# Moving the capacity mask of a routed MLP three tiles later, and laying its one-hots out with the token column innermost

## The reference, cut to what matters

```python
xn  = layernorm(x)                                   # x: 16 x 512 x 256
h   = scan(lam, xn @ B_w.T)                          # state space layer, 64 states
aff = xn @ waff.T / (|xn| * |waff|)                  # 8 experts
cap = clip(floor(S * sigmoid(mean(aff) - threshold)), 4, S)
top = one_hot(argmax(aff))                           # each token has one expert ...
kept = rank of the token in its expert's row < cap   # ... which keeps only its best cap tokens of a batch row
for each expert e:  out += gelu((xn * mask_e) @ W1[e] + b1[e]) @ W2[e] + b2[e]   # for ALL tokens
y = x + (h @ C_w.T + D * xn) + out
```

## Time and profile before

| what | value |
|---|---|
| time, median of 3 runs | 661.86 us (659.16 to 662.46) |
| the profiled execution | 663.84 us, its span 662.1 us |
| PE busy | 589.7 us (89%) |
| DVE busy | 512.2 us (77%) |
| POOL busy | 462.6 us (70%) |
| ACT busy | 337.3 us (51%) |

### The profile page before, as it was taken

One profiled execution on the slowest core, in us unless ns is written; L12 is line 12 of the kernel. 1 busy time (PEld: TensorE's weight loads), 2 busy tenths in 40 slices (PEclk: granted clock), 3 DMA queues, 4 the chain that ended last, 5 costly groups with the idle time before them and its releaser, 6 DMA issues.

```text
span 662.1 us, 16027 instructions
## 1 busy us (share of the span) xinstructions
PE 589.7 (89%) x4597; PEld 497.0 (75%) x4598; DVE 512.2 (77%) x974; ACT 337.3 (51%) x635; POOL 462.6 (70%) x625
## 2 busy tenths in 40 slices
PE   2988888858945599999999999999999999999994
PEld 1655555546834499898988888989898989898983
DVE  5789989799998979987667768676767676767672
ACT  5776868825799235644433435353535353535340
POOL 1999997920038838888776768787777787788453
PEclk9988868776997799999999999999999999999998
DMA  8985757611801134512212112212112212210100
GB/s 308 413 346 173 253 208 266 230 75 43 274 18 33 40 97 153 169 57 74 72 57 70 54 53 66 75 50 79 49 44 71 67 48 67 63 60 24 51 29 2
DMA packets 33584, 72.58 MB, mean 110 GB/s; under 512 B 6519, under 2 KB 19088, under 8 KB 33552
## 3 DMA queue, kind: packets, MB, share of 16 engines
q1 hardware_dynamic: 21488, 46.67, 19.7%
q0 software_dynamic: 11232, 25.20, 12.4%
q10 hardware_dynamic: 832, 0.31, 0.2%
HBM read 50.64 MB, written 27.00 MB: 117 GB/s over the span
## 4 chain that ended last, share of the span: by engine, by line
PE 69%; DVE 16%; ACT 7%; issue 6%; DMA 1%; POOL 1%; DVEq 0%; SPq 0%; ACTq 0%; POOLq 0%
PE ps_bu L820 10%; PE ps_bu L818 10%; PE ps_bu L819 10%; PE ps_t L793 5%; PE ps_y L795 5%; PE ps_t L794 5%; PE ps_y L794 5%; PE ps_t L795 5%; PE ps_y L793 5%; ACT area L494 2%; PE ps_y L662 2%; PE ps_bu L648 2%; PE ps_t L630 2%; ACT work L565 1%; PE ps_g L777 1%
## 5 line engine op out<-in xcount | busy, mean ns | idle before, releaser
L820 PE MATMUL ps_bu<-area,ring 128*128 x624 | 170.1, 273 | 1.5 <-issue 1.4
L818 PE MATMUL ps_bu<-area,ring 128*128 x624 | 170.1, 273 | 0.3
L819 PE MATMUL ps_bu<-area,ring 128*128 x624 | 170.1, 273 | 0.0
L1247 DVE SCALAR_TENSOR_TENSOR ring<-ring,h_scale 128x512 f16<-128x512 f32 x156 | 117.2, 751 | 5.6
L434 POOL DMA_INDIRECT out<-ring,idx_b x78 | 96.9, 1243 | 19.1 <-issue 14.7
L372 POOL TENSOR_TENSOR small<-ones 128x1 f32<-128x1 f32 x156 | 48.1, 308 | 86.8 <-DVE work L1161 33.4
L420 POOL DMA_INDIRECT work<-xn_rows,idx_x x78 | 87.1, 1117 | 27.1 <-issue 23.9
L444 POOL DMA_INDIRECT work<-base_rows,idx_b x78 | 92.3, 1183 | 18.0 <-issue 15.8
L596 ACT ACTIVATE ring<-ps_t,b1t,inv_in 128x256 f32<-128x256 f32 x156 | 79.2, 560 | 44.7 <-PE ps_t L795 42.4
L596 ACT ACTIVATE ring<-ps_y,b1t,inv_in 128x256 f32<-128x256 f32 x156 | 77.8, 562 | 45.9 <-PE ps_y L795 22.8
L1244 DVE TENSOR_SCALAR ring<-ring,h_scale 128x512 f16<-128x512 f32 x156 | 77.9, 499 | 23.4 <-issue 13.2
(11 more groups left out here) (267 smaller groups left out, 1085.0 us busy)
## 6 DMA issues: line engine op xcount, KB each, us to landing
ring<-L_ffn_W SPq DMA_DIRECT2D x14, 1024.0 KB, 6.4
xn_rows<-area SPq DMA_DIRECT2D x8, 1024.0 KB, 9.4
base_rows<-area SPq DMA_DIRECT2D x8, 1024.0 KB, 7.3
area<-L_attn_u SPq DMA_DIRECT2D x7, 1024.0 KB, 18.2
work<-L_ffn_W SPq DMA_DIRECT2D x5, 1024.0 KB, 9.0
work<-xn_rows,idx_x POOLq DMA_INDIRECT x78
work<-base_rows,idx_b POOLq DMA_INDIRECT x78
out<-ring,idx_b POOLq DMA_INDIRECT x78
```

The lines of the kernel that those rows point to most:

```text
L818: t.matmul(dst, hh, wh, start=(c == 0), stop=False)
L819: t.matmul(dst, hh, wl, start=False, stop=False)
L820: last = t.matmul(dst, hl, wh, start=False, stop=(c == C - 1))
L1247: v.scalar_tensor_tensor(out=hlo[p][:, cs], in0=h32[:, cs], scalar=h_scale[:, bass.ds(e, 1)], in1=hhi[p][:, cs], op0=ALU.mult, op1=ALU.sub ...
```

## The change

1. One-hots are stored with the token column innermost (128 x l x 16 in place of 128 x 16 x l), compared against a replicated counter `irep` that POOL writes once, and all operands are 16-bit. PE reads them with a stride of 16 elements (32 bytes).
2. The first affinity work is in another order: PE turns the affinity rows first, DVE makes the search key ahead of the one-hot of the expert, and PE computes zero rows 0 and 1 ahead of the count products.
3. The second key of the search is made by POOL. Tables of ACT are asked for ahead by two 128x1 ACTIVATEs.
4. ACT's second search is interleaved: after turn 4 three `zero_rows` copies, after turn 5 `split_x` of tile 0 and the last copy, after turn 7 all of step 0, after turn 9 all of step 1.
5. `result` is cut in two: `drained` (L1255) and the rest. Tiles 0 to 2 are drained unmasked; `kept_rows` stands in step 3 and `kept_slots` at its end, the mask is there in step 4. The late W2 units are split in steps 4 to 7 and not 2 to 5.
6. Their DMAs wait for `slots_ok` and not for `mask_ok`. `PEEL` is 10. Two low parts (units 10 and 11) come after the largest values of units 12 to 15.

```diff
-        lo16 = part(area, (UNITS - 4) * UW, T * P // 2).bitcast(F16).rearrange("p (t l) -> p t l", l=P)
+        lo16 = [part(area, (UNITS - 4) * UW + n * TG * P // 2, TG * P // 2).bitcast(F16).rearrange("p (l t) -> p l t", t=TG)
+                for n in range(4)]
...
-                    last = t.matmul(ps_num[:, g * NS:(g + 1) * NS], lo16[:, g * TG + i, :], planes[g][:, i, :],
+                    last = t.matmul(ps_num[:, g * NS:(g + 1) * NS], lo16[g][:, :, i], planes[g][:, :, i],
...
-                link(v.tensor_tensor(planes[g], same(NS), of(hi16, NS), ALU.is_equal))
+                link(v.tensor_tensor(planes[g], irep[:, 0:NS, :], of(hi16[:, cols], NS), ALU.is_equal))
...
+            pool.wait_ge(s["low_ok"], 1)
+            pool.wait_ge(s["hi_found"], 1)
+            g.tensor_scalar(search[:, 4:5], search[:, 0:1], -1.0, None, ALU.mult)
+            link(g.tensor_scalar(key_hi, key_hi, search[:, 0:1], 2.0 ** 17, ALU.add, ALU.mult))
+            g.memset(search[:, 0:1], -(2.0 ** 15 - 0.5))
+            g.tensor_tensor(key_hi, key_hi, low_half, ALU.add).then_inc(s["key_lo_ok"], 1)
...
+            for m in range(5, 8):
+                gates = rows_in(m, m % 4, gates)
+            for m in range(5, 8):
+                gates = out_and_base(m - 5, m - 3, (m + 3) % 4, (m + 1) % 4, gates)
...
             def second_half(n):
-                if n == 8:
-                    for i in range(E // 2):
+                if n == 4:
+                    for i in range(3):
                         zero_rows(i)
-                if n == 10:
+                if n == 5:
                     split_x(0, 0)
+                    zero_rows(3)
+                if n == 7:
+                    act.wait_ge(s["wsum_ok"], UNITS)
+                    act.wait_ge(s["scales_ok"], 1)
+                    step(0, 0)
+                if n == 9:
+                    step(1, 1)
...
             zero_row(0)
             zero_row(1)
             pe.wait_ge(s["oh_ok"], 1)
...
                 up(j, p)
-                if isinstance(j, int) and j == 0:
+                if first == 0:
                     late_bounds()
+                if first == 3:
                     kept_rows()
-                if isinstance(j, int) and j == 1:
+                if first == 4:
+                    pe.wait_ge(s["mask_ok"], 1)
+                    rows_t(5, 1, 2)
+                if first > 0:
+                    down(j - 1, 1 - p)
+                if first == 3:
+                    pe.wait_ge(s["kept_read"], 1)
+                    rows_t(4, 0, 2)
                     kept_slots()
-                if not (isinstance(j, int) and j == 0):
-                    down(j - 1, 1 - p)
...
+            x_low(1, 1)
+            h_parts(0, 0)
+            late_scales()
+            x_low(2, 0)
+            h_parts(1, 1)
+            out_scales()
+            drained(0, 0)
+            x_low(3, 1)
+            kept()
+            h_parts(2, 0)
+            drained(1, 1)
+            kept_places()
+            x_low(4, 0)
+            h_parts(3, 1)
+            kept_mask()
+            dve.wait_ge(s["mask_ok"], 1)
+            dve.wait_ge(s["c_ok"], E)
+            result(0, 0, 0)
+            result(1, 1, 0)
+            drained(2, 0)
```

More of the change, by code:

```diff
@@ L407, in is_tile, with rows_in, out_and_base @@
                 return not isinstance(j, int) or 0 <= j < NT
[L409 to L424, removed]
+            def rows_in(m, r, gate_no):
+                wait(pool, s["f_xt"], m - 1)
+                gate(gate_no)
+                g.tensor_copy(idx_x[:, 2 * r:2 * r + 2], idx_all[:, bass.ds(m * 2, 2)]).then_inc(s["ix"], 1)
+                pool.wait_ge(s["ix"], m + 1)
+                gate(gate_no + 1)
+                for h in range(2):
+                    g.indirect_dma_start(out=xg[r % 2][:, h * D:(h + 1) * D], out_offset=None, in_=xn_dram,
+                                         in_offset=bass.IndirectOffsetOnAxis(
+                                             ap=idx_x[:, 2 * r + h:2 * r + h + 1], axis=0),
+                                         bounds_check=bound, oob_is_err=False).then_inc(gx[r % 2], 16)
+                return gate_no + 2
+            def out_and_base(t_out, t_base, ro, rb, gate_no):
                 if is_tile(t_out):
@@ L599, in step @@
             def step(j, p):
[L600 to L604, removed]
+                if isinstance(j, int) and j in (3, 4):
+                    hidden(j)
+                    split_x(j + 1, 1 - p)
+                else:
+                    split_x(j + 1, 1 - p)
+                    hidden(j)
+                if isinstance(j, int) and 4 <= j < 4 + LATE:
+                    act.wait_ge(s["w_late"], 16 * (j - 3))
+                    high_part(EARLY + j - 4, raw_late)
             act.wait_ge(s["key_hi_ok"], 1)
@@ L703, in _ @@
             pe.wait_ge(s["affsum_ok"], 1)
[L704 to L710, removed]
-            states_out(B - 1)
+            t.matmul(ps_num[:, AFF_AT:AFF_AT + 1], ones[:], small[:, 16:17], start=True, stop=True).then_inc(s["aff_t"], 1)
+            states_out(B - 2)
             def zero_row(e):
@@ L1002, in denominators @@
                 link(v.reciprocal(rden, den))
+            order, first = small[:, 40:48], small[:, 81:85]
             for b in range(B):
@@ L1161, in _ @@
             v.tensor_copy(idx_all, iv).then_inc(s["idx_ok"], 1)
-            largest(14)
-            low_part(10, raw[2])
-            low_part(11, raw[3])
+            for n in (14, 12, 13):
+                largest(n)
             def kept():
@@ L1272, in step @@
             def step(j, p, k):
-                first = isinstance(j, int) and j == 0
-                second = isinstance(j, int) and j == 1
                 x_low(j + 1, 1 - p)
-                if first:
-                    kept()
                 h_parts(j, p)
-                if first:
-                    kept_places()
-                    late_scales()
-                if second:
-                    kept_mask()
-                    out_scales()
-                    dve.wait_ge(s["c_ok"], E)
-                if isinstance(j, int) and 2 <= j < 2 + LATE:
-                    low_part(EARLY + j - 2, raw_late)
-                if not (isinstance(j, int) and j < 1):
-                    result(j - 1, 1 - p, k - 1 + p)
+                if isinstance(j, int) and j < 4 + LATE:
+                    low_part(EARLY + j - 4, raw_late)
+                drained(j - 1, 1 - p)
+                result(j - 1, 1 - p, k - 1 + p)
             tile_scales()
             x_low(0, 0)
-            for n in (12, 13, 15):
-                largest(n)
-            for j in range(PEEL):
+            largest(15)
+            low_part(10, raw[2])
+            low_part(11, raw[3])
+            x_low(1, 1)
[18 more added lines that the diff above has]
+            drained(2, 0)
+            x_low(5, 1)
+            h_parts(4, 0)
+            low_part(EARLY, raw_late)
+            result(2, 0, 1)
+            drained(3, 1)
+            x_low(6, 0)
+            h_parts(5, 1)
+            low_part(EARLY + 1, raw_late)
+            result(3, 1, 1)
+            drained(4, 0)
+            result(4, 0, 2)
+            for j in range(6, PEEL):
                 step(j, j % 2, j // 2)
```

164 lines of the change are left out of this document (85 added, 79 removed).

## The result

The changed kernel takes **669.5 us** (669.0 to 670.2) where the kernel before takes 661.4 beside it: ratio 1.0128, 95% interval 1.0099 to 1.0156. It is slower by 1.3%; 652 and "faster" were forecast. The profiled execution of the changed kernel took 669.2 us, its span is 667.5.

A forecast was written before the change was run, and what follows sets the result against it. The prediction took PE to bound the tiles at 10.92 us each, leaving only the stretch before step 5 to gain. Its terms, -2.9 - 9.1 + 2.0 = -10.0 us, gave 652 us, range 644 to 660 (about 0.8).

The forecast's parts named there:

- What bounds it: Loop tiles: PE bounds them at 10.92 us each, unchanged, so only the stretch from 145 us to step 5 counts.
- One-hots on DVE: half, 2.5 us a group: Before the index: 16-bit packed operands cut a group of one-hots on DVE from 5.1 to 2.5 us.
- Rival (b): One-hots on DVE do not get faster: +5.5 us, 657.5; chance 0.09.
- A strided product: 0.095 us: PE's one-hot products with both operands strided by 32 bytes: 0.095 us each, bounds 0.037 and 0.26.
- The index gains nothing: Front, up to the slots' index: PE's order and strided reads take DVE's gain; index at 191.5, before 191.74.
- From the index to `up(0)`: -2.9: Gathers of the first tiles: low parts moved later free POOL, so `up(0)` starts at 201.9, 2.9 us earlier.
- From `up(0)` to step 5: -9.1: First steps on PE: fewer waits for mask and one-hots, 58.9 us in place of 67.9, another 9.1 us gained.
- Behind step 5: +2.0: Handover to the loop: held-back results, POOL's backlog and late W2 units cost 2.0 us together.
- rival (d): Handover to the loop stalls on late W2 units and POOL's backlog, or ACT's `step(1)`: +6 to +8, 659; chance 0.13.
- (c): PE's strided reads are dear: gain used up at 0.173 us a product, 673 us at 0.26; chance 0.10.
- The sum: Whole kernel: -2.9 - 9.1 + 2.0 = -10.0 us, so 652 us forecast.

The follow-up runs named there:

- e5: Changed kernel with both one-hots packed again and each small value stored twice, so DVE's innermost axis is a pair: 650.1 us, ratio 0.9834.
- e13: Kernel of e5 without POOL's scatters of results 0 to 2 and DVE's waits for them: 644.2 us, ratio 0.9742.
- e14: Kernel of e5 without DVE's low parts of the late W2 units; ACT writes a scaled copy instead: 646.6 us, ratio 0.9787.
- e15: Kernel of e5 without the scatters of results 0 to 2 and without DVE's late low parts: 641.5 us, ratio 0.9733.
- e12: Kernel of e5 unchanged, measured once more as a repetition: 652.6 us, ratio 0.9878.
- e1: Changed kernel with both one-hots back in the old packed layout, all else as changed: 662.2 us, ratio 1.0031.
- e9: Kernel of e1 plus ten groups of 32 products at various strides behind the last tile; 678.5 us in one run, only the added groups read.
- e3: Kernel of e1 with the moving columns (`planes`) left strided and the weights packed: 670.7 us, ratio 1.0143.
- e2: Kernel of e1 with the weights (`lo16`) left strided and the moving columns packed: 660.5 us, ratio 0.9997.
- e4: Kernel before the change with nothing but the new strided one-hot layout: 669.9 us, ratio 1.0138.
- e7: Kernel before the change with nothing but the stored pairs, one-hots packed: 654.9 us, ratio 0.9908.

## Why the prediction was wrong, step by step

**What bounds it** held: the last 26 tiles took 283.8 us in every kernel but the profile of before (286.6), and apart from where they begin only the three stretches differ.

**One-hots on DVE: half, 2.5 us a group.** Right: 0.80 + 1.23 + 0.80, less overlap 2.7. The Trainium skill's condition ("VectorE: DVE Perf Modes", What auto-detection actually checks) agrees with the rows: 16-bit with a step of one gives 1.23 us for 2048 elements, the repeated value with a step of zero 2.29. Rival (b) is out.

**A strided product: 0.095 us.** This is the step that failed. It is 0.148 to 0.149. The prediction took "a strided column costs about 1 ns" from a 32-bit weight load and applied it to moving columns; the moving column at 32 bytes costs 0.143 / 78 = 1.8 ns. The price for 128 products is (0.148 - 0.095) x 128 = 6.8 us more than in the sum. Second, the sum had no term for the clock, which falls in the strided products: zero row 4 behind the first group took 5.22 us in place of 3.69, 1.5 more, and from the first matmul of `up(4)`, which began at 0.50, to step 5 PE took 13.3 us (261.61 to 274.89) in place of the 10.9 of e5, 2.4 more. Changed against e5, the stride costs 62.72 - 53.70 = 9.0 us in the first stretch and 64.83 - 55.63 = 9.2 in the second, 18.2 in all, of which 128 x (0.148 - 0.037) = 14.2 are the products themselves and 4.0 are left for the clock, as the 1.5 and 2.4 say. The prediction had 7.4.

**The index gains nothing.** It lost: it came at 199.99, where 191.5 was forecast and 191.74 was the kernel before; 2.5 us of that is the later start of the stretch. DVE's tile table was done at 186.3 and the fourth group of products at 197; the whole of DVE's gain went into an 11 us wait for PE. With the pairs this stretch is 6.3 us shorter than before.

**From the index to `up(0)`: -2.9.** Right: before, POOL had the index at 191.74 and `up(0)` started 13.0 later; after, these are 199.99 and 210.06, 10.1 apart. The four gathers of the first two tiles took 1.0 to 1.3 us each, with DVE's low parts gone from beside them, and not 2.78.

**From `up(0)` to step 5: -9.1.** The order does what it was said to do. (The prediction's own terms sum to 58.9 against 67.9, which is 9.0 and not 9.1, and on PE's timeline the old stretch is 67.7; it changes nothing here.) With products at the packed price the prediction's own working gives -9.1 - 3.7 = -12.8; e5 measured 55.63 - 67.73 = -12.1. What the strided products and the clock took of it (9.2, 3.7 of them counted) left -2.9. No wait of `kept_rows` or `x_low` for ACT's interleaved search came: PE waited 0.87 us for the masked one-hots, 1.0 was reckoned.

**Behind step 5: +2.0.** Too small by 5.4: steps 5 to 10 took 72.87 and not 65.5, 7.4 more than at PE's pace. The prediction reckoned POOL's round at 10.2 us against PE's 10.92 from rows of the running loop and let the backlog be worked off beside it. Beside each of the four late low parts, though, POOL is held for some 2 us, so the round is longer than PE's tile just while the three scatters are to be made up (e13, e14, e15). This was rival (d), which came true almost in full (5.4 for its 6 to 8), and beside it a part of (c). (c)'s point of reversal, 0.173 us, was reckoned for the product's price alone and was not reached; at 0.148 the kernel is slower because the clock (4) and the handover (5.4) came on top.

**The sum.** Forecast -10.0. Products +6.8, clock +4, handover +5.4 make +6.2; the medians differ by +8.1. The 2 us left are not explained; two measurements of one kernel, e5 and e12, differ by 2.5 in their medians.

**Left open:** whether e1 would be ahead of before without the stall of steps 5 to 10. By the table it would (7.6 us lost there), but no run shows it. A version that keeps the late mask and avoids the stall with the full output was not found; by the third stretch of e15, which leaves work out, it would be worth at most another 8 us. Why a wide moving stride lowers the clock while PE is busy is not shown either, only that it does.

## What to carry to other kernels

A layout has two readers. Before turning a tile round for DVE's doubled rate, price PE's side by its moving columns, at their own stride and number: here the four groups of one-hots became 2.4 us shorter each on DVE, and the products cost PE 14 us more, and 4 through the clock. Often the fast rate can be had without the turn, since a pair of neighbouring elements is enough. And an engine whose round just fits the tile time (10.2 of 10.92) has little room for postponed work; look at what holds it in exactly those rounds, not in the steady loop.

## What the runs showed of the hardware that was not expected

- **Moving columns, 16 bit:** 0.45 ns a column at a step of 2 bytes, 0.47 at 4, 0.93 at 8, 1.8 at 16 and 32 (e9, 78 columns; the clock was 1.00 up to 8 bytes, 0.86 at 16 and 0.50 at 32, and e3 has the same 1.8 at 32 bytes at 1.00). The dear strides cost the same at either level of the clock.
- **Weights, 16 bit:** a step of 16 or 32 bytes makes a product of 78 packed columns 0.060 to 0.062 us and not 0.035 to 0.037 (e9, clock 0.96; e2, clock 1.00). Steps of 4 and 8 bytes were measured at 0.50 only, where they cost no more than packed weights. In the changed kernel the strided load of 128 columns is recorded with 148 ns in place of 98.
- **The clock fell under strided products** with PE at 9.95 of 10 us busy: 0.71 in that stretch and 0.50 in the 3 us behind it, while packed products at the same place kept it at 1.00 (e5). In e9 it fell with PE busy all the time; in e4 four groups of 16 between zero rows did not lower it.
- **A pair is enough for DVE's doubled rate:** innermost axis of two elements, the axis around it repeated with a step of zero: 128x2048 in 1.22 to 1.30 us (e7, e5) against 2.29.
- **POOL stands still beside DVE's low part:** 2.0 to 2.2 us for an addition of 128x1 that takes 0.20, ending with it (e5: 257.94 + 2.20 and 257.75 + 2.35). The low part reads two tensors of SBUF, one of them 32 bit. The Trainium skill ("SBUF — State Buffer", Who interferes with whom) says that a DVE instruction with two SBUF inputs contends with a GpSimd instruction that reads SBUF; the rows agree.
